# Attention inside a macaron block: denominators one pair later, output projection before the turn, the maxima spread on ScalarE

## What is computed

```python
x = x + 0.5 * ffn(layernorm(x))          # shared experts + top-2 of 8 routed experts
x = x + attention(layernorm(x))
x = x + 0.5 * ffn(layernorm(x))
```

```python
q, k, v = split(x @ w_qkv.T)
q = q * cos + rotate_half(q) * sin + fenc       # k likewise
attn = softmax(einsum(q, k) * 64 ** -0.5)
out = einsum(attn, v).reshape(b, n, 1024) @ w_out.T + b_out
```

## Time and profile before

| | |
|---|---|
| median of 3 runs | 1263.31 us (1261.71 to 1264.05) |
| the profiled execution: its own time / its span | 1261.11 us / 1259.3 us |
| busy: TensorE, VectorE, GpSimd, ScalarE | 97%, 76%, 72%, 50% |
| granted TensorE clock, mean | 1.00 |
| attention, 64 periods | from about 236 to 1052 us of the span |

### The profile page before, as it was taken

The page is one execution under the profiler, slowest core; times in us unless marked ns, Lnnn a source line. Parts: engine busy times, 40 slices in busy tenths (PEclk is TensorE's granted clock), DMA queues, the critical chain, the costliest instruction groups (busy, mean ns, idle before and its releaser), DMA issues.

```text
span 1259.3 us, 20278 instructions
## 1 busy us (share of the span) xinstructions
PE 1221.0 (97%) x7346; PEld 764.9 (61%) x7346; DVE 955.4 (76%) x1439; ACT 628.5 (50%) x921; POOL 905.0 (72%) x652
## 2 busy tenths in 40 slices
PE   5999999899999999999999999999999999999998
PEld 3666666456665656565666666665656555666665
DVE  6665687778888888888888889788878866666632
ACT  3444532456555555546555555555655554443422
POOL 0444347688898999898899889899989862543443
PEclk9999999999999999999999999999999999999999
DMA  5351241123232323233232323232323221443140
GB/s 171 135 185 50 86 142 27 34 52 69 55 74 52 77 52 73 56 69 60 62 68 60 69 60 70 52 77 53 73 56 71 58 44 20 142 143 112 40 160 17
DMA packets 118674, 95.30 MB, mean 76 GB/s; under 512 B 75760, under 2 KB 85008, under 8 KB 118320
## 3 DMA queue, kind: packets, MB, share of 16 engines
q1 hardware_dynamic: 118064, 93.75, 30.2%
q10 hardware_dynamic: 512, 0.26, 0.1%
HBM read 57.53 MB, written 2.88 MB: 48 GB/s over the span
## 4 chain that ended last, share of the span: by engine, by line
PE 80%; DVE 6%; POOL 5%; issue 5%; ACT 2%; DMA 1%; SPq 0%; DVEq 0%; POOLq 0%; ACTq 0%
PE banks L1177 16%; PE banks L1154 13%; PE banks L455 12%; PE banks L468 8%; PE banks L1086 6%; PE banks L1006 5%; PE banks L1194 5%; PE banks L1159 4%; PE banks L1204 4%; PE banks L1014 3%; POOL work L1452 2%; POOL turn L1442 1%; PE banks L1129 1%; DVE side_turned L702 1%; POOL turn L1436 1%
## 5 line engine op out<-in xcount | busy, mean ns | idle before, releaser
L1018 DVE TENSOR_REDUCE neg_max<-banks 128x2 f32<-128x1024 f32 x256 | 301.7, 1226 | 13.3 <-PE banks L1006 9.2
L1281 ACT ACTIVATE work<-banks 128x1024 f32<-128x1024 f32 x256 | 262.4, 1026 | 88.3 <-PE banks L1159 64.8
L1177 PE MATMUL banks<-work 128*64 128x512 f32 x1024 | 233.8, 598 | 0.0
L1452 POOL TENSOR_TENSOR work<-work 128x1024 f32<-128x1024 f32 x64 | 161.4, 2521 | 62.4 <-PE banks L1177 62.4
L1442 POOL TENSOR_TENSOR turn<-turn,side_turned 128x512 f32<-128x512 f32 x128 | 170.9, 1355 | 30.8 <-DMA side_turned<-side 30.7
L1436 POOL TENSOR_TENSOR turn<-turn,fenc 128x512 f32<-128x512 f32 x128 | 163.0, 1294 | 2.0 <-DVE side L1352 2.0
L1447 POOL TENSOR_TENSOR qk_l<-turn,qk_h 128x512 fp32r<-128x512 f32 x128 | 162.0, 1288 | 2.8 <-ACT qk_h L995 2.8
L1177 PEld LDWEIGHTS banks<-work 128*64 128x64 f32 x1024 | 67.8, 136 | 132.6 <-issue 130.8
L1373 DVE TENSOR_TENSOR work<-work 128x1024 f32<-128x1024 f32 x64 | 108.2, 1690 | 35.0 <-PE banks L1177 34.7
L816 POOL TENSOR_TENSOR o_raw<-o_raw,work 128x512 f32<-128x512 f32 x52 | 67.1, 1292 | 87.7 <-DVE o_raw L734 80.6
L995 ACT ACTIVATE qk_h<-turn 128x512 fp32r<-128x512 f32 x128 | 80.6, 631 | 89.5 <-POOL turn L1442 89.4
(11 more groups left out here) (178 smaller groups left out, 2441.9 us busy)
## 6 DMA issues: line engine op xcount, KB each, us to landing
work<-share SPq DMA_DIRECT2D x32, 1024.0 KB, 9.4
side_turned<-side SPq DMA_DIRECT2D x256, 128.0 KB, 3.2
rec_all<-rec_d SPq DMA_DIRECT2D x128, 128.0 KB, 2.9
x_tok<-in_x SPq DMA_DIRECT2D x8, 256.0 KB, 6.2
out<-x_tok SPq DMA_DIRECT2D x8, 256.0 KB, 9.5
work<-in_w_gate_up SPq DMA_DIRECT2D x1, 1280.0 KB, 7.0
work<-in_w_qk SPq DMA_DIRECT2D x1, 1024.0 KB, 11.8
den_d<-den_rows ACTq DMA_DIRECT2D x64, 4.0 KB
```

Of the source, the lines that this page charges most:

```text
L1018: return nc.vector.tensor_reduce(neg_max[:, g % 2, qt::DH], of, AX.X, ALU.max, negate=True)
L1177: ins = nc.tensor.matmul(o_bank(g)[OWN[h], :], v_all[:, kt, n * DH:(n + 1) * DH], pt[:, g % 2, kt, h * T:(h + 1) * T], start=(kt == 0), st ...
L1281: nc.scalar.activation(pt[:, g % 2, kt, :], S[kt].rearrange("p h q -> p (h q)"), ACT.Exp, scale=QSCALE).then_inc(s["probs"], 1)
L1452: nc.gpsimd.tensor_tensor(pt[:, g % 2, 2, :], pt[:, g % 2, 2, :], pt[:, g % 2, 3, :], ALU.add).then_inc(s["second_sum"], 1)
```

## The change

Eight things are edited together:

1. `apply_v` goes through the key tiles in the order 2, 3, 0, 1.
2. The sums change sides: VectorE adds tiles 2 and 3 (`late_sum`) as soon as these two have been applied; GpSimd adds 0 and 1 into tile 3's place (`early_sum`) afterwards.
3. `denominators` runs one pair later (p-2), straight behind `apply_v`, into bank 5. `project_out` runs one pair later too (p-4), behind it and in front of `turn_maxima`. `o_raw` gets a third buffer.
4. The spreading of the maxima leaves VectorE (one instruction) for ScalarE (four instructions of 128x128, with a scale per partition), between the copy of the denominators and the copy of the values.
5. The copy of the denominators on ScalarE moves from in front of the exponentials to behind the copy of the output.
6. `rope` is cut in two parts: keys as soon as the keys are projected, then queries, two instructions of 128x512 each.
7. Reciprocals and their transfers run one pair later, the residual stands in front of `rope`, and waits are changed to fit.
8. After the last period there is now one pair more to finish: two reciprocals stand between "experts" and "masks", and `project_out(N - 3)` moves from unit 0 to unit 3.

```diff
 def denominators(g, p):
-    pe.wait_ge(s["v_ready"], min(p + 4, B * 2 * TT))
+    if den_bank(g) is W:
+        pe.wait_ge(s["v_ready"], B * 2 * TT)
+        pe.wait_ge(s["maxes"], N * TT)
     if not steady(p):
         at_least(pe, s["den_copied"], g)
-    pe.wait_ge(s["first_sum"], g + 1)
-    pe.wait_ge(s["second_sum"], g + 1)
+        pe.wait_ge(s["late_sum"], g + 1)
+    pe.wait_ge(s["early_sum"], g + 1)
...
 def period(p):            # TensorE
     if exists(last):
-        for kt in range(TT):
+        for kt in ORDER:
             apply_v(last, kt)
+    if exists(p - 2):
+        denominators(p - 2, p)
+    if exists(p - 4):
+        project_out(p - 4, p)
     if exists(nxt):
         turn_maxima(nxt, p)
...
     if value_tile(p):
         values(p)
-    if exists(p - 3):
-        project_out(p - 3, p)
...
-    if exists(last) and p != JOIN_LOGITS_AT:
-        denominators(last, p)
...
+def spread_maxima(g):      # ScalarE
+    act.wait_ge(s["shift_ps"], g + 1)
+    at_least(act, s["scores"], (g - 1) * TT)
+    for t in range(TT):
+        ins = nc.scalar.activation(shift[:, g % 2, t * P:(t + 1) * P], MT, ACT.Copy, scale=own_rows[:, t:t + 1])
+    ins.then_inc(s["shift_ready"], 1)
...
 def period(p):            # ScalarE
-    if exists(p - 2):
-        copy_den(p - 2)
...
         copy_o(last)
+    if exists(p - 2):
+        copy_den(p - 2)
...
         x_high(front_at(p))
+    if exists(p + 1):
+        spread_maxima(p + 1)
     if value_tile(p):
         copy_values(act, p)
...
 def rope(g):              # VectorE
-    dve.wait_ge(s["qk_ps"], g + 1)
     at_least(dve, s["low"], g - 1)
     dve.wait_ge(s["turned"], 64 * g)
-    for to, part in ((turn[:, g % 2], 0), (side[:], 1)):
-        ins = nc.vector.tensor_tensor(to, KQ, rope_t[:, part:part + 1, :].broadcast_to([P, QK, T]), ALU.mult)
+    for part, done in ((K, s["k_ps"]), (Q, s["qk_ps"])):
+        dve.wait_ge(done, g + 1)
+        nc.vector.tensor_tensor(turn[:, g % 2, part], KQ[:, part, :], rope_t[:, 0, :], ALU.mult)
+        ins = nc.vector.tensor_tensor(side[:, part], KQ[:, part, :], rope_t[:, 1, :], ALU.mult)
     ins.then_inc(s["roped"], 1)
...
 # VectorE after the last period
     ffn2["vector"](dve, "experts")
+    reciprocals(N - 3)
     reciprocals(N - 2)
     ffn2["vector"](dve, "masks")
...
 # SyncE after the last period
-den_in(N - 2)
-reciprocals_out(N - 2)
-reciprocals_in(N - 2)
+for g in (N - 3, N - 2):
+    den_in(g)
+    reciprocals_out(g)
+    reciprocals_in(g)
 den_in(N - 1)
```

More of the change, by code:

```diff
@@ L907, in steady, with den_bank @@
             def steady(p):
-                return TT <= p < N - 3
+                return TT + 1 <= p < N - 3
+            def den_bank(g):
+                return bank[5] if own_bank(g + 1) else W
             def exists(g):
@@ L1193, in denominators @@
                                 c, first = 32 * (2 * h + a), h * T + a * HALF
-                                ins = nc.tensor.matmul(W[c:c + 32, 0:HALF], ones_f[:],
-                                                       pt[:, g % 2, kt, first:first + HALF], start=(n == 0), stop=(n == 1))
+                                ins = nc.tensor.matmul(den_bank(g)[c:c + 32, 0:HALF], ones_f[:],
+                                                       pt[:, g % 2, kt, first:first + HALF], start=(kt == 2), stop=(kt == 3))
                     ins.then_inc(s["den_ps"], 1)
@@ L1260, in pe @@
                     ffn2["tensor"](pe, "turn")
-                    for kt in range(TT):
+                    for kt in ORDER:
                         apply_v(N - 1, kt)
                 elif tail == 0:
-                    project_out(N - 3, N)
+                    project_out(N - 4, N)
                 elif tail == 1:
                     denominators(N - 1, N)
+                elif tail == 3:
+                    project_out(N - 3, N)
                 elif tail == 5:
@@ L1359, in maxima @@
                     maxima_of(g, qt, M[qt]).then_inc(s["maxes"], 1)
-                def spread_maxima(g):
-                    dve.wait_ge(s["shift_ps"], g + 1)
-                    at_least(dve, s["scores"], (g - 1) * TT)
-                    spread(g, MT).then_inc(s["shift_ready"], 1)
                 def reciprocals(g):
@@ L1396, in period @@
                             maxima(nxt, qt)
-                    if exists(p - 2):
-                        reciprocals(p - 2)
+                    if exists(p - 3):
+                        reciprocals(p - 3)
                     end_norm(p)
@@ L1458, in normalise @@
                     at_least(pool, s["y_ps"], g - 1)
[L1459 removed]
+                    nc.gpsimd.tensor_tensor(o_t[:, g % 2], o_raw[:, g % 3], rec_all[:, g % 2],
                                             ALU.mult).then_inc(s["o_ready"], 1)
```

91 lines of the change are left out of this document (48 added, 43 removed).

## The result

| | before | after | forecast |
|---|---|---|---|
| median | 1263.68 us (4 runs) | 1301.99 us (1301.39 to 1303.88, 4 runs) | 1300 (1272 to 1318) |
| ratio to before | | 1.0305, 95% interval 1.029 to 1.0319 | 1.029 |
| profiled execution: own time / span | 1261.11 / 1259.3 us | 1302.26 / 1300.5 us | 1298.6 own time |
| busy: TensorE, VectorE, GpSimd, ScalarE | 97, 76, 72, 50% | 95, 70, 72, 53% | |

The account below looks back on a forecast made before the run. It took TensorE to bound the kernel, busy 656.3 of 660 us mid-attention. Terms -6 + 12.5 + 4.5 + 10 + 6 + 7.5 + 3 = +37.5 us on 1261.1 gave 1298.6, forecast as a 1300 us median; range 1272 to 1318.

Parts of the forecast that it names:

- Two chains outgrow TensorE's period: Ordinary periods: VectorE's third maxima late by 0.07 to 0.1 us; ScalarE's chain to block 2 12.26 us against 11.8.
- The rival in which ScalarE has room: Attention periods: GpSimd's Q is not held, so ScalarE's chain fits; 1285 us in all, chance 0.25.
- The size in the middle: Ordinary attention periods: +12.5 us over 50 periods, VectorE's 4 us inside it; ends 4 and 28 us.
- Late by 0.07 to 0.1: VectorE's first reduction reaches the third maxima at +3.98 against +3.91 in every period; 4 us over 50 periods.
- 0.25 x 50: ScalarE's chain is short by 0.45 us, shared by two periods, plus slower transfers: 12.5 us, VectorE's 4 included.
- Four spreading instructions: ScalarE's spreading of the maxima takes 1.25 us for all four, between 1.0 and 1.64 us.
- Periods with a new batch: Seven periods before a front lose 0.65 us each, 4.5 in all; seven with a front 1.4 each, 10 in all.
- Removed waits, -6: TensorE's waits for denominators, and for the output projection in the last two periods, go: gain of 4 to 8 us.
- The last two periods: Second block's token instructions and high parts precede ScalarE's spreading; block 2 waits about 3.8 and 2.1 us: +6 us.
- Behind the last period: Two reciprocals in a row before the masks hold VectorE 7.5 us; slow TensorE products after the pause add 3 us.
- Faster: Rival: values product runs into the denominators without a shape jump, gaining 0.1 us a period; 1260 us, chance 0.06.
- The clock: Rival: TensorE pausing in many middle periods falls to half rate for stretches, costing 10 us; 1310 us, chance 0.04.

Follow-up runs that it names:

- e3: Changed kernel with the output projection back behind the values tile on TensorE and the residual back behind the rotation on VectorE: 1285.96 us.
- e2: Changed kernel with ScalarE issuing the denominators' transfer behind the spreading, and spreading before the second block's tokens and high parts in the last periods: 1290.46 us.
- e4: Changed kernel with the spreading of the maxima back on VectorE, one instruction between the late sum and the residual: 1310.44 us.
- e5: Changed kernel with the rotation whole again, two instructions over keys and queries together once the queries are projected: 1326.69 us.
- e7: Kernel before with swapped sums, denominators through residual one pair later at their old places in the period, and N-3's reciprocals before the second block's logits: 1262.02 us.
- e1: Changed kernel with the reciprocals of pair N-3 in front of the last late sum instead of behind "experts": 1295.99 us.
- e11: Kernel before with swapped sums and the pair later alone, the logits' turn earlier, and pair N-3's denominators also behind the second block's logits: 1262.73 us.

## Why the prediction was right, step by step

**Two chains outgrow TensorE's period: right.** e3 gives both their cover back and the floor returns to 12.68. e2 shortens only ScalarE's and the waits of block 2 go. e4 (which shortens ScalarE's) and e5 lengthen VectorE's and every period grows. Both waits, block 2's and that of the third maxima, stand where the forecast looked for them, and a third, block 3 for the rotation, is in no step of it. The rival in which ScalarE has room described most periods better than the forecast, and still did not give its time.

**The size in the middle: right by two errors.** "Late by 0.07 to 0.1" of the third maxima was too small. In e2, where nothing else waits, a period takes 12.88 against 12.68. Of these 0.2 us the late reduction is 0.16: the spacing from one product to the next is 0.28 in place of 0.23 us in front of the third maxima, and then 0.33 in place of 0.23 behind them. These are medians; one period of e2 and one of the kernel before show it, the third maxima in the middle of each:

```profile
661.69 0.39 PE L1164 MATMUL banks<-shift,ones_r 64*128 64x512 f32 x2
661.99 0.50 PE L1011 MATMUL banks<-qk_h 64*128 64x512 f32 x2
662.33 0.40 PE L1159 MATMUL banks<-qk_h 64*128 64x512 f32 x2
```

```profile
707.35 0.40 PE L1159 MATMUL banks<-shift,ones_r 64*128 64x512 f32 x2
707.58 0.40 PE L1006 MATMUL banks<-qk_h 64*128 64x512 f32 x2
707.82 0.40 PE L1154 MATMUL banks<-qk_h 64*128 64x512 f32 x2
```

The step left out the second part, the wider spacing to the product behind a late weight load. The other 0.04 lie in the new order of shapes (a term of 0 in the forecast); in e3, with the projection back, they are gone. Against this, ScalarE's chain was priced too dear: "0.25 x 50" less VectorE's 4 is 8.5 us. Of the 11.7 us in the ordinary periods about 8.4 come from the floor (42 x 0.2) and 5.5 from block 2 (15 periods, 0.37 each; e2 gave back 5.3), less the 2.3 us of removed waits. So the total of the middle came out by luck: VectorE's chain was priced at about half of its cost, ScalarE's at one and a half times. The link from the end of the rotation to the turned half had been read from one period (5.28 against 5.18 in over half of them). That ScalarE does not go on while it issues a transfer was read from the earlier trace rows, where the row's own mark names the scores as what ended the wait. The changed kernel bears it out for instructions behind the issue (0.62 us), e2 shows that those in front of it run on.

**Four spreading instructions: right.** 1.25 us forecast from the earlier trace rows, 1.14 measured. The Trainium skill (ScalarE: Activation LUTs, What ACT_TABLE_LOAD costs) gave an estimate of 1.27, which the trace undercuts by a tenth.

**Periods with a new batch: tokens right, fronts too dear.** Tokens 5.1 against 4.5. Fronts 6.4 against 10: the delay of x_high behind the denominators' transfer was smaller: in the front at 399 us x_high started at 399.96, the front's products having ended at 399.89, and the rotation at 401.21, 0.8 us behind the first query product where the step has 1.5. The step also named the wrong wait. Block 3 waits for the rotation before the third maxima can:

```profile
403.74 0.50 PE L1159 MATMUL banks<-qk_h 64*128 64x512 f32 x2 [0.16 <-DVE side L1375]
```

**Removed waits, -6: the step that failed (+1.3 in the first four periods).** What it says of the middle holds: the kernel before averaged 12.73 us in ordinary periods against its floor of 12.68, 2 us in 42, and they are gone (inside the 11.7 above). The first two periods gained 0.45 and 0.67 us. But the next two lost 0.56 and 1.88. I had priced the waits that go in the first and the last periods, and not those that come there: outside the steady middle `project_out` also waits for the output copy of its own period, and it now stands 1.0 us (the denominators) behind the product that this copy reads, while ScalarE is still at the high part of Q.

```profile
292.53 1.13 PE L1212 MATMUL banks<-wo,o_t 128*128 128x128 f32 x8 [1.02 <-ACT o_raw L1318]
```

**The last two periods: the mechanism right, both waits a little shorter.** The forecast has two waits of block 2, 3.8 and 2.1 us, behind ScalarE's token instructions and its high parts. They came with 3.22 and 1.77 us. The second begins behind the last turn, so the table counts it there. The +5.5 of the table are the first wait with slow products behind it, and a wait that was not in the sum: the projection waited for the output copy again, 1.71 us. In e2, which spreads before that work, the waits for the spreading fell to 0.81 and 0.36 us (one of 1.48 us for an exponential came up in between).

```profile
1045.83 1.13 PE L1212 MATMUL banks<-wo,o_t 128*128 128x128 f32 x8 [1.71 <-ACT o_raw L1318]
...
1050.72 0.80 PE L1159 MATMUL banks<-qk_h 64*128 64x512 f32 x2 [3.22 <-ACT shift L1312]
...
1065.50 0.50 PE L1159 MATMUL banks<-qk_h 64*128 64x512 f32 x2 [1.77 <-ACT shift L1312]
```

**Behind the last period: the stand right, its after-effect too dear.** The stand was 7.7 us against 7.5. The after-effect of the pause was smaller than the 3 us taken: the products ran at 0.63 us from 1099.0 to 1102.2, which costs 1.3. These two and the 1.77 us of block 2 come near the table's 10.9, but the account isn't closed: the last period's projection and denominators (some 2 us) stand behind the last turn before the change and in front of it after, and the extra pair costs something too (e7), which was not in the sum.

**The sum.** 1300 against 1302 is in part luck. The removed waits were 7.3 us too hopeful in the first periods, the fronts 3.6 too dear, and the two chains of the middle wrong in opposite directions. (The ends 1269 and 1326 were left on the profiled execution's own time; with the 2.2 us that the forecast adds they are 1271 and 1328.)

**Faster: not so.** Its condition was that the values product runs into the denominators with no jump. The spacing there is 0.52 us, where two products with the values are 0.42 apart, so the jump of 0.1 exists.

**The clock.** The rival's mechanism exists, at the end and not in the middle. Granted clock of three stretches of the changed kernel (columns as in the earlier trace rows): a middle one, behind the 3.2 us wait, and behind the 9.6 us stop.

```profile
1036.00:1046.00 10.00, 8.29 (x63) 4.03 (x60) 6.32 (x6) 6.05 (x8) 8.69 (x6) 1.00 0.32 54
...
1049.00:1054.00 5.00, 3.28 (x16) 2.63 (x18) 0.74 (x1) 2.69 (x7) 1.43 (x2) 0.50 0.07 4
...
1099.00:1102.00 3.00, 2.96 (x15) 2.15 (x16) 2.16 (x6) 0.60 (x1) 0.00 (x0) 0.50 0.08 27
```

0.50 is the 1.2 GHz level. In the middle, where TensorE waited for up to 1.0 us at a time, the clock stayed at 1.00. That such waits can't lower it elsewhere is not shown.

## What to carry to other kernels

A busy share of 97% on the bounding engine says nothing about how far the others are from binding: count each chain from the place where TensorE releases it to the place where TensorE needs it, and know which products lie between, since these are its cover. Moving 0.9 us of products out of that gap cost 16 us (e3), more than the order on ScalarE (11.5, e2) or the two reciprocals in a row (6, e1). In a list that is served in order, an instruction that waits for a transfer must not stand in front of work that another engine needs; it held VectorE for 7.7 us in the change and for 1.7 us again in a repair of mine.

## What was new about the hardware

- A weight load that moved its product by about 0.06 us cost TensorE 0.16 us in all: the spacing behind that product was 0.33 instead of 0.23 us too (the medians of 41 periods of e2 against 31 of the kernel before).
- Issuing a transfer directly behind the ScalarE instruction that it waits for made ScalarE stand 0.62 us; with four short instructions between them in the list the issue (0.48 us) ran beside these.
- After a stop TensorE's products of 128x512 took 0.63 us in place of 0.40 for a while, and the stretch was not equally long behind like stops. It was 3.6 us behind a wait of 3.22 in the changed kernel, but 6.2 us in e1, which is the same up to there (clock 0.62 over the stretch below, of which the last 1.8 us ran at full rate); 3.1 us behind the stop of 9.62 in the changed kernel, 6.3 us behind one of 9.42 in e2. In the first pair the clock was at 0.50 from 1047.6 to 1054.2 us in both; what differs is how much of that the stop covered. In e7 a stop of 1.99 us was followed, 0.8 us later, by 3.4 us at the low level; in e11 a stop of 1.64 us by none.

```profile
1048.50:1056.00 7.50, 7.50 (x42) 5.34 (x42) 3.79 (x4) 3.50 (x4) 0.00 (x0) 0.62 0.01 2
```

```profile
1057.77 0.50 PE L455 MATMUL banks<-x_hi,gu_hi 128*128 128x512 f32 x1 [1.99 <-DVE work L734]
...
1059.54 0.63 PE L455 MATMUL banks<-x_hi,gu_lo 128*128 128x512 f32 x1
```

- Behind the first long pause of the program the same slow products ran while the window view prints a granted clock of 1.00 for 16 to 22 us. There the duration of the product tells more than the clock column.
